# Graph stage: GpSimd's addition into X, whole at the head of its step or in four parts between the scatters

## The reference, cut to what matters

```python
x = x + _L0_gnn_ref(_layernorm(x), adj, ...)   # attention over adj, then an MLP
x = x + _L0_ffn_ref(_layernorm(x), ...)        # attention over slices
x = x + _L1_gnn_ref(_layernorm(x), ...)        # two graph convolutions
x = x + _L1_ffn_ref(_layernorm(x), ...)        # mixture of experts, 2 of 8, and a shared one
```

```python
out = x @ w_root + b + (einsum('bij,bid->bjd', mask, x) / deg) @ w_rel[1]
h = elu(out)
```

## Time and profile before

| | before |
|---|---|
| median of 3 runs | 3112.45 us (3101.8 to 3119.04) |
| the profiled execution | 3107.38 us |
| its span, first to last instruction | 3105.7 us |
| mean granted clock of TensorE | 0.924 |
| busy share: PE, PEld, DVE, ACT, POOL | 88, 72, 63, 48, 45% |
| scatters of the graph stage, L1241 | 256, 251.0 us busy, mean 981 ns |
| scatters of the expert stage, L1845 | 288, 283.5 us busy, mean 984 ns |

### The profile page before, as it was taken

The page is one execution under the profiler, slowest core; times in us unless marked ns, Lnnn a source line. Parts: engine busy times, 40 slices in busy tenths (PEclk is TensorE's granted clock), DMA queues, the critical chain, the costliest instruction groups (busy, mean ns, idle before and its releaser), DMA issues. The chain is left out here.

```text
span 3105.7 us, 86211 instructions
## 1 busy us (share of the span) xinstructions
PE 2724.5 (88%) x28365; PEld 2226.0 (72%) x28366; DVE 1951.2 (63%) x6886; ACT 1483.5 (48%) x2992; POOL 1405.5 (45%) x2060
## 2 busy tenths in 40 slices
PE   8999999899799999999996766666657999999798
PEld 4666665799577777777775756655646888888687
DVE  5666665677778888888883666666643444444332
ACT  3444444555456656655663444444423444444343
POOL 4555553333233333333332555555650555555543
PEclk8999999999899999999997777677768999999899
DMA  1111111000000000000000111111411222222254
GB/s 47 34 34 34 33 31 27 1 0 0 1 0 0 0 0 0 0 0 0 0 0 22 37 46 41 39 43 41 127 35 42 71 73 77 75 76 70 71 156 134
DMA packets 158079, 117.85 MB, mean 38 GB/s; under 512 B 20151, under 2 KB 145594, under 8 KB 158011
## 3 DMA queue, kind: packets, MB, share of 16 engines
q1 hardware_dynamic: 140602, 81.02, 9.5%
q0 software_dynamic: 17408, 35.95, 3.4%
HBM read 68.36 MB, written 48.56 MB: 38 GB/s over the span
## 5 line engine op out<-in xcount | busy, mean ns | idle before, releaser
L781 POOL TENSOR_TENSOR s_sw<-s_expo,s_rsum 128x512 f32<-128x512 f32 x128 | 133.5, 1043 | 492.2 <-DVE s_rsum L1026 492.2
L1867 ACT ACTIVATE e_hidden<-e_ps,e_b1g 128x512 f32<-128x512 f32 x288 | 191.0, 686 | 282.4 <-PE e_ps L61 161.2
L1845 POOL DMA_INDIRECT token_y<-e_y,e_rows x288 | 283.5, 984 | 78.0 <-issue 68.5
L1241 POOL DMA_INDIRECT sorted_z<-r_z,r_rows x256 | 251.0, 981 | 86.4 <-issue 86.4
L1901 PE MATMUL e_ps<-expert_w,e_hidden 128*128 x2304 | 282.0, 275 | 3.6 <-issue 3.6
L1901 PEld LDWEIGHTS e_ps<-expert_w,e_hidden 128*128 128x128 f32 x2304 | 274.8, 192 | 9.9 <-issue 3.7
L427 DVE TENSOR_REDUCE a_V<-a_ps_s 128x8 f32<-128x1024 f32 x128 | 157.0, 1226 | 179.0 <-PE a_ps_s L366 179.0
L291 ACT ACTIVATE a_probT<-a_ps_st 128x1024 f32<-128x1024 f32 x128 | 131.1, 1024 | 204.9 <-PE a_ps_st L374 204.9
L366 PEld LDWEIGHTS a_ps_s<-a_nT 16*128 16x128 f32 x2048 | 137.2, 189 | 92.3 <-issue 56.3
L366 PE MATMUL a_ps_s<-a_nT 16*128 16x128 f32 x2048 | 186.8, 301 | 11.3
L1942 DVE TENSOR_TENSOR e_biased<-e_ps,expert_b 128x512 f32<-128x512 f32 x72 | 49.8, 692 | 231.9 <-remote 172.2
(11 more groups left out here) (398 smaller groups left out, 8171.3 us busy)
## 6 DMA issues: line engine op xcount, KB each, us to landing
e_z<-sorted_z SPq DMA_DIRECT2D x72, 260.0 KB
c_y<-token_y SPq DMA_DIRECT2D x22, 512.0 KB, 4.0
X<-in_x_dram SPq DMA_DIRECT2D x32, 256.0 KB, 2.8
a_adj<-in_adj_dram SPq DMA_DIRECT2D x32, 256.0 KB, 2.8
g_adj<-in_adj_dram SPq DMA_DIRECT2D x32, 256.0 KB
out_dram<-X SPq DMA_DIRECT2D x32, 256.0 KB
c_y_s<-token_y SPq DMA_DIRECT2D x10, 512.0 KB
token_y<-e_y,e_rows POOLq DMA_INDIRECT x288
```

The lines of the kernel that those rows point to most:

```text
L781: nc.gpsimd.tensor_tensor(sw[p][:, :, :], expo[p][:, :, :], rsum[p][:, 1, :].unsqueeze(2).to_broadcast([T, HEADS, C]), ALU.mult).then_inc( ...
L1241: nc.gpsimd.indirect_dma_start(sh.sorted_z, bass.IndirectOffsetOnAxis(ap=rows[p][:, e * GB + b:e * GB + b + 1], axis=0), zr[p][:, b, e, :] ...
L1845: nc.gpsimd.indirect_dma_start(sh.token_y, bass.IndirectOffsetOnAxis(ap=rows[p][:, b:b + 1], axis=0), y[p][:, b, :], None).then_inc(y_scat ...
L1867: nc.scalar.activation(hidden[p][:, c, :], ps_1[c % 2][:, :], ACT.Gelu, bias=b1g[p][:, c:c + 1]).then_inc(s["hidden_done"], 1)
```

## The change

GpSimd's step no longer begins with the addition. The addition of group t - 3 is made in four instructions, one for each graph, 128 elements per partition each. The scatters' order is changed so that both choices of one graph are sent together, and the addition for graph `piece` stands behind the two scatters of graph `piece` (they belong to different groups, t - 6 and t - 3, and share no data). The wait on `elu2_done` stands ahead of the first part, the signal `x_done` is given by the fourth. Steps without scatters make the four additions in a row, behind the inverse deviations.

```diff
             def step(t, r, p, known):
-                if live(known, 3, groups):
-                    pool.wait_ge(s["elu2_done"], t - 2)
-                    at = X[:, bass.ds((t - 3) * GB, GB), :]
-                    nc.gpsimd.tensor_tensor(at, at, elu2[1 - p][:, :, :], ALU.add).then_inc(s["x_done"], 1)
                 measured = live(known, 0, groups) or live(known, 4, groups)
...
-                if live(known, 6, groups):
+                adds, scatters = live(known, 3, groups), live(known, 6, groups)
+                if scatters:
...
-                    for e in range(2):
-                        for b in range(GB):
+                for piece in range(GB):
+                    if scatters:
+                        for e in range(2):
                             nc.gpsimd.indirect_dma_start(
-                                sh.sorted_z, bass.IndirectOffsetOnAxis(ap=rows[p][:, e * GB + b:e * GB + b + 1], axis=0),
-                                zr[p][:, b, e, :], None).then_inc(scattered[p], 16)
+                                sh.sorted_z,
+                                bass.IndirectOffsetOnAxis(ap=rows[p][:, e * GB + piece:e * GB + piece + 1], axis=0),
+                                zr[p][:, piece, e, :], None).then_inc(scattered[p], 16)
+                    if adds:
+                        if piece == 0:
+                            pool.wait_ge(s["elu2_done"], t - 2)
+                        at = X[:, bass.ds((t - 3) * GB + piece, 1), :].squeeze(1)
+                        last = nc.gpsimd.tensor_tensor(at, at, elu2[1 - p][:, piece, :], ALU.add)
+                if adds:
+                    last.then_inc(s["x_done"], 1)
```

## The result

The forecast held. The median of the changed kernel is 3074.6 us (3070.8 to 3082.3, four runs) against 3115.3 us of the kernel before beside it (3101.8 to 3119.0, four runs): a ratio of 0.990, 95% interval 0.988 to 0.993, 1.0% faster. The prediction was 3065 us, range 3038 to 3118. The profiled execution took 3074.4 us (span 3072.7) where the kernel before took 3107.4: 33 us less, two thirds of the 48 that the sum gave.

What follows compares the result with a forecast made beforehand. Signals held during GpSimd's scatter bursts bound the graph stage; 24 periods falling from 19.17 to 16.8 us save 56.9, ends lose 2.6 and 6.0, together -48.3: 3059 us profiled, 3065 us median forecast, range 3038 to 3118.

Steps and rivals of the forecast that it cites:

- the sum: Graph stage: -56.9 us over 24 periods, +2.6 and +6.0 at two losing places, together -48.3 us.
- What bounds it: Graph stage: TensorE's signals are held during long scatter bursts until something drains; L1641 starts 4.2 us late.
- Head addition removed: GpSimd's step head, L1216: VectorE's statistics cover the addition, so removing it is worth nothing.
- Quarter additions: GpSimd's burst: 0.46 us each, pauses of 0.81 us (0.65 to 1.05), last scatter 1.5 us later.
- threshold of 0.63: Pause between scatter pairs: a pair's backlog is empty if the pause is at least 0.63 us.
- The loop: Graph stage, L1555 to L1225 to last scatter to `x_done`: new period 16.8 us (16.3 to 17.7).
- The ends: Graph stage's steps 6 to 8 and 32 to 35 lose +2.6 and +6.0 us.
- A: Graph stage: pauses free nothing, holds last to the burst's end; slower, 3157 us or 3143; chance 0.17.
- B: Graph stage: holds remain in part or the loop is longer; period 18.5 to 19.2, 3105 to 3121 us; 0.13 including C.
- C: GpSimd's scatter gaps hide the quarter additions, so burst and holds stay; 3112 us; chance counted with B, 0.13 together.
- The rule on the port: On-chip memory: only GpSimd and VectorE contend, TensorE never waits; by it the 4.2 us would have another cause.

Runs made afterwards that it cites:

- e4_short_pauses: Kernel before with scratch additions of 8 elements behind the second, fourth and sixth scatter; 2972.0 us against 2965.3, ratio 1.002, on a chip without holds.
- e5_again: Kernel before with one scratch addition of 128 elements behind the fourth scatter, on a chip with holds; 3058.1 us against 3112.0, ratio 0.983.
- e1_pauses_only: Kernel before with scratch additions of 128 elements behind the second, fourth and sixth scatter; 2982.1 us against 2965.3, ratio 1.005, on a chip without holds.
- e6_early_signal: Changed kernel with its addition parts one place earlier, `x_done` ahead of the last scatter pair; 2975.0 us against the kernel before's 2965.3, ratio 1.003.
- c1_change: Changed kernel as it is, against the kernel before on chip 7, without holds; 3038.2 us against 2964.2, ratio 1.025.

## Why the prediction was right

**What bounds it.** Right for the chip of the result: signals are held during long bursts, 90 in before; in after 7 are left, none of them in a burst with parts in it. What I had taken for a property of the kernel goes with the chip: five others show no hold. The trace of one chip could not tell it, and that the result was measured where signals are held is luck: chip 7 would have given 74 us more instead of 41 less.

**Head addition removed: nothing.** Right: GpSimd waits 2 us for VectorE's means where the addition was.

**Quarter additions.** 0.46 us was right where VectorE left them alone (0.46 to 0.48); beside some of VectorE's work they took up to 0.68, twice 0.80, and the average of all is 0.526. The gap behind them was 0.16, not 0.30 us, so a pause without company is 0.02 + 0.46 + 0.16 = 0.64 to 0.65, the lower end of my range, and by my own threshold of 0.63 a near thing. It was enough in every burst that had parts. The threshold itself is not tested, since e4_short_pauses never met a chip with holds. The burst, from first scatter to last record, became 11.33 or 11.69 us in place of 9.87: +1.46 or +1.82, where I had 1.5.

**The loop.** Right in kind and near in size: L1561 to L1221 1.86 us (forecast 1.84), L1221 to the end of the last scatter 14.36 or 14.72 (14.41), last addition and signal 0.64 (0.56). A period is 16.86 or 17.23 in turn, with two longer ones, and 17.12 on average against 16.8. Over 24 periods: 410.9 us where 403.2 was forecast. This is the first mis-sized term, 7.7 us. VectorE's wait for `x_done` was to be about 1 us a step; it is 1.9 on average, mostly 0.65 and 2.72 in turn.

**The ends.** GpSimd's rows of the same four steps in after, for the earlier trace rows:

```profile
1736.53 0.20 POOL L1221 TENSOR_TENSOR g_rstd<-g_meanvar,eps 128x8 f32<-128x8 f32 x1 [11.94 <-DVE g_meanvar L1571]
...
1770.84 0.21 POOL L1221 TENSOR_TENSOR g_rstd<-g_meanvar,eps 128x8 f32<-128x8 f32 x1 [2.02 <-DVE g_meanvar L1571]
...
2181.74 0.21 POOL L1221 TENSOR_TENSOR g_rstd<-g_meanvar,eps 128x8 f32<-128x8 f32 x1 [1.53 <-DVE g_meanvar L1571]
...
2233.60 0.21 POOL L1221 TENSOR_TENSOR g_rstd<-g_meanvar,eps 128x8 f32<-128x8 f32 x1 [1.53 <-DVE g_meanvar L1571]
```

Steps 6 to 8: 34.3 us, +3.3 (forecast +2.6). Steps 8 to 32: -49.2 (-56.9). Steps 32 to 35: 51.9, +7.4 (+6.0). Two stretches were not in the sum: steps 0 to 6, +2.0, and from step 35 to the stage's end, +4.4. Together -32.1, the stage's -32.0. Whether these two are the change's work is open: on chip 7 the same stretches differ by -1.3 and -0.5 (78.2 and 76.9, 98.6 and 98.1 us). The rest of the execution gave +5.7 in the expert stage and -3.9 and -2.7 in attention and slices, none of them touched by the change.

**The rivals.** A is out by the trace of after: L1647 no longer follows the burst's end. Its outcome, slower, is what the chips without holds show, by another way: not that the pauses free nothing, but that there is nothing to free. The price is higher than my +45 us: 24 x (17.08 - 14.69) = 57 us in the steps 8 to 32 and 74 us in the median, since the new loop is set against a period of 14.69, which no row of the first trace had shown. B's period of 18.5 did not come. C is out by the rows: the pauses are there.

**The rule on the port.** The Trainium skill, SBUF — State Buffer, section "SBUF: two separate sides", says that TensorE never waits on anyone there. The traces of chip 7 agree, with no signal of TensorE's held in either kernel; where there is a hold it is the signal that comes late (4.2 us in the earlier trace rows) behind a matmul that has ended, so the runs don't contradict the rule.

**What stays open.** Where the queue is that holds the signals, what ends a hold (see e5_again), and why chips 5, 7, 15, 2 and 8 show none and 13 and the chip of the result do (whether these are one and the same is not known, nor whether a chip keeps its state). The shortest pause that frees: e1_pauses_only, e4_short_pauses and e6_early_signal never met a chip with holds. By the prices above, e6's order (three pauses, `x_done` early: +7 to +10 us without holds) looks better than the change on either kind of chip, and e5's single pause (+2 us without, 3058.1 in one run with) looks the safest; only the latter was seen to beat the change, by 16 us, between two results that may be of two chips, and in one run. No version beat the kernel before where nothing is held.

## What to carry to other kernels

An idle engine whose releaser is named "remote", or a transfer that ended long ago, while GpSimd issues indirect transfers, deserves a look at the true last signal: its matmul may have ended microseconds earlier. Breaking the burst frees such signals, but whatever is used to break it should not move a signal that another engine waits for to the burst's far end: here that one edit alone cost 62 us where nothing was held, and the whole change 74. And a change that cures a stall should be timed on more than one chip before it is kept; the cure's own price shows only where the stall doesn't occur.

## What the hardware showed that I had not expected

- The same kernel takes 2965 us on five chips (2964.2 to 2965.5 in their medians) and 3112 on a sixth, as in the runs of the result (3115). Of the 142.1 us between the profiled spans of the two (3105.7 and 2963.6), 113.6 lie in the graph stage and 24.6 in the expert stage, the two stages with bursts of indirect transfers; attention, MLP and slices differ by at most 2.1 us each.
- Holds outlive the change: in the expert stage of after 237 of 385 updates are still held, and the stage takes 537.6 us where c1_change, without holds, has 507.0.
- With holds, the release times in a burst are not free: counted from the burst's start most fall near 4.2, 5.7, 7.1, 7.8, 8.5, 9.9, 10.6 and 11.4 us, multiples of about 0.71, half of the 1.43 us that the prediction read for a scatter. These too are worked out from the semaphore records of before and e5_again.
- GpSimd's gap behind a small addition that was queued ahead is 0.16 to 0.17 us (87 gaps of after, 57 of them 0.16); behind a scatter it is 0.30.
